# Two mixture-of-experts layers around attention: keeping the split weights of experts 11 to 15 in SBUF during the first layer

## What is computed

```python
x = x + 0.5 * moe(layernorm(x), norm_w, gate_w, gate_b, w1, b1, w2, b2)
x = x + attention(layernorm(x), w_q, w_k, w_v, w_o)
x = x + 0.5 * moe(layernorm(x), norm_w, gate_w, gate_b, w1, b1, w2, b2)

def moe(x, ...):                     # x: 2048 tokens of 256
    t = x * rsqrt(mean(x * x) + eps) * norm_w
    vals, idx = top_k(t @ gate_w.T + gate_b, 4)
    G = softmax(vals) scattered into (tokens, 16)
    h = einsum('mh,eoh->emo', t, w1) + b1        # 512 columns
    a, b = minimum(h[..., ::2], 7), clip(h[..., 1::2], -7, 7)
    act = a * sigmoid(1.702 * a) * (b + 1)       # 256 columns
    y = einsum('emi,edi->emd', act, w2) + b2     # 256 columns
    return x + einsum('me,emd->md', G, y)
```

## Time and profile before

| | us |
|---|---|
| median of 3 runs | 806.96 |
| lowest and highest run | 806.67, 808.38 |
| the profiled execution | 809.67 |
| its span in the profile | 807.9 |
| TensorE busy | 703.2 |
| VectorE (DVE) busy | 585.3 |
| ScalarE (ACT) busy | 439.8 |
| GpSimd (POOL) busy | 402.4 |

### The profile page before, as it was taken

One profiled execution on the slowest core, in us unless ns is written; L12 is line 12 of the kernel. 1 busy time (PEld: TensorE's weight loads), 2 busy tenths in 40 slices (PEclk: granted clock), 3 DMA queues, 4 the chain that ended last, 5 costly groups with the idle time before them and its releaser, 6 DMA issues.

```text
span 807.9 us, 17709 instructions
## 1 busy us (share of the span) xinstructions
PE 703.2 (87%) x4754; PEld 558.6 (69%) x4754; DVE 585.3 (72%) x1324; ACT 439.8 (54%) x1066; POOL 402.4 (50%) x449
## 2 busy tenths in 40 slices
PE   2576558989999999778999999998699999999995
PEld 1453336768888888666677777656478888888872
DVE  2868356877777777647779888857777777777777
ACT  3663334555555555426667676655345555555551
POOL 6667764445555555453234532447525555555552
PEclk9999978999999999999999999989999999999999
DMA  7779899998888773265444344137656778877676
GB/s 296 271 270 370 271 328 330 406 377 278 250 273 270 248 238 100 99 234 179 162 147 175 135 148 149 60 127 256 224 185 233 268 252 270 267 240 239 225 259 241
DMA packets 87420, 188.88 MB, mean 234 GB/s; under 512 B 13072, under 2 KB 37920, under 8 KB 85792
## 3 DMA queue, kind: packets, MB, share of 16 engines
q1 hardware_dynamic: 47680, 102.31, 37.4%
q0 software_dynamic: 14928, 49.97, 16.3%
q10 hardware_dynamic: 24720, 35.47, 13.4%
HBM read 105.46 MB, written 65.45 MB: 212 GB/s over the span
## 4 chain that ended last, share of the span: by engine, by line
PE 26%; POOL 11%; issue 10%; DVE 7%; DMA 1%; ACT 1%; SPq 0%; ACTq 0%; DVEq 0%; POOLq 0%
POOL kbuf L1283 6%; PE s_psT L1071 5%; PE s_psO L1656 3%; PE s_psS L1621 3%; DVE s_a_nm L1889 2%; PE s_psG L1593 2%; POOL rows L1514 2%; POOL s_e_own_bc L1295 2%; PE s_psG L1095 2%; PE s_psT L1637 1%; PE s_psT L1641 1%; PE s_psG L1606 1%; PE s_psG L1703 1%; PE s_psS L1038 1%; PE s_psG L1679 1%
## 5 line engine op out<-in xcount | busy, mean ns | idle before, releaser
L1283 POOL DMA_INDIRECT kbuf<-f_e_ys,f_e_place x79 | 79.2, 1003 | 99.0 <-ACT f_e_ys L1230 78.3
L1283 POOL DMA_INDIRECT kbuf<-s_e_own_ys,s_e_own_place x79 | 79.0, 1000 | 91.7 <-ACT s_e_own_ys L1230 78.7
L1071 PE MATMUL f_bank<-f_e_w,f_e_th 128*128 x316 | 121.1, 482 | 3.5 <-ACT f_e_th L1255 2.6
L1071 PE MATMUL s_psT<-s_e_own_w,s_e_own_th 128*128 x316 | 113.7, 461 | 2.0 <-ACT s_e_own_th L1255 1.8
L1514 POOL DMA_INDIRECT rows<-s_a_row,s_a_slot_i x64 | 63.7, 995 | 77.5 <-DVE s_a_slot_i L2016 60.5
L1889 DVE TENSOR_REDUCE s_a_nm<-s_psS 128x4 f32<-128x1024 f32 x64 | 78.2, 1222 | 27.1 <-PE s_psS L1621 26.8
L1136 DVE TENSOR_TENSOR s_e_own_hb<-s_psT,s_e_own_bias 128x512 f32<-128x512 f32 x79 | 54.3, 687 | 48.4 <-PE s_psT L1071 48.4
L1136 DVE TENSOR_TENSOR f_e_hb<-f_bank,f_e_bias 128x512 f32<-128x512 f32 x79 | 54.2, 687 | 45.4 <-PE f_bank L1071 45.3
L657 POOL DMA_INDIRECT rows<-f_r_row,f_r_slot_i x64 | 67.5, 1054 | 35.5 <-issue 17.9
L1071 PEld LDWEIGHTS f_bank<-f_e_w,f_e_th 128*128 128x128 f32 x316 | 63.3, 201 | 25.7 <-issue 7.4
L2155 ACT ACTIVATE s_a_pT<-s_psT 128x1024 f32<-128x1024 f32 x62 | 63.3, 1022 | 31.1 <-PE s_psT L1641 31.0
(11 more groups left out here) (383 smaller groups left out, 1804.7 us busy)
## 6 DMA issues: line engine op xcount, KB each, us to landing
f_e_w<-w_split SPq DMA_DIRECT2D x24, 512.0 KB, 5.1
...
s_e_tb<-rows ACTq DMA_DIRECT2D x80, 144.0 KB, 3.3
w_split<-stage ACTq DMA_DIRECT2D x7, 1536.0 KB, 7.8
f_e_tb<-rows ACTq DMA_DIRECT2D x66, 144.0 KB, 4.9
...
w_split<-stage POOLq DMA_DIRECT2D x5, 1536.0 KB, 7.3
...
```

What stands on the lines that cost most here:

```text
L1071: last = pe.matmul(psH[j][:, :], left[:, p % 2, j, k * P:(k + 1) * P], w1[:, bass.ds(buf, 1), h, k * I2:(k + 1) * I2], start=n == 0, stop= ...
L1283: pool.indirect_dma_start(out=kbuf[:, :], out_offset=bass.IndirectOffsetOnAxis(ap=place[:, i % KEPT:i % KEPT + 1], axis=0), in_=ys[:, n, : ...
```

## The change

Experts 11 to 15 are no longer reloaded in the first layer. They are loaded raw into places where they stay, split there, and used from there. All weights of the first layer lie in one array `weights` of 28 units of 1024 columns: nine units that were the three stage buffers, 13 of the ring, and six kept ones, which share their memory with the router's buffers. Experts 11 and 12 stay in stage buffers 1 and 2, 13 and 14 in the kept units, 15 in stage buffer 0. In the second layer the array has only the 13 ring units.

The five experts are still stored, since the second layer reads them, but at POOL's steps 16, 19, 22, 25 and 28 instead of 4, 6, 8, 9 and 11. The raw loads of 13 and 14 wait for no store now, that of 15 for the store of 10. SP waits at its end for the five stores, ahead of the fetch of the attention weights, which land in the ring's memory. Weight loads that were two DMAs are one.

The table's column with the expert's number now holds a packed word: the expert, the unit of its first weights shifted by 5, and that of its second weights shifted by 10. DVE computes it as a sum over steps. TensorE unpacks it with shifts and masks.

```diff
+UNIT = 1024
+SLOT, RING_UNITS, HOME_UNITS = 3, 13, 6
+RING_AT, KEPT_AT = 3 * SLOT, 3 * SLOT + RING_UNITS
+UNITS = KEPT_AT + HOME_UNITS
+SECOND_UNITS = (2, 5, 8, 11, 12)
+HOMES = {11: SLOT, 12: 2 * SLOT, 13: KEPT_AT, 14: KEPT_AT + SLOT, 15: 0}
+def spots(first_layer):
+    base = RING_AT if first_layer else 0
+    return [(HOMES[e], HOMES[e] + 2) if first_layer and e in HOMES else (base + SLOT * (e % 4), base + SECOND_UNITS[e % 5]) for e in range(NE)]
+def packed(first_layer):
+    return [e + (first << 5) + (second << 10) for e, (first, second) in enumerate(spots(first_layer))]
...
+    one.done(one.engine.tensor_tensor(tiles["passed"][:, :], tiles["past"][:, :], steps, ALU.mult))
     one.link(one.engine.tensor_tensor(tiles["pastn"][:, :], tiles["past"][:, :], tiles["nt"][:, :], ALU.mult))
+    one.done(one.engine.tensor_reduce(tiles["spot"][:, :], tiles["passed"][:, :], X_AXIS, ALU.add))
...
-        one.done(one.engine.tensor_copy(table[0:1, to:to + NT], psN[0:1, k * P:k * P + NT]))
+        one.done(one.engine.tensor_scalar(table[0:1, to:to + NT], psN[0:1, k * P:k * P + NT], float(first) if k == 1 else 0.0, None, ALU.add))
...
+    BEHIND = {7: 4, 8: 5, 9: 6, 10: 7, 11: 8, 12: 9, 15: 10}
...
     def load(self, queue, e):
-        if e - self.STAGED >= self.DIRECT:
-            queue.wait_ge(self.s_out[e - self.STAGED - self.DIRECT], 16)
-        if e >= self.DIRECT:
-            queue.dma_start(self.staged(e)[:, 1, :].bitcast(fp32), self.w_raw[e]).then_inc(self.s_in[e], 16)
-        else:
-            queue.dma_start(self.ring1[:, e, 1, :].bitcast(fp32), self.w_raw[e, :, 0:HID]).then_inc(self.s_in[e], 16)
-            queue.dma_start(self.ring2[:, e, 1, :].bitcast(fp32), self.w_raw[e, :, HID:WCOLS]).then_inc(self.s_in[e], 16)
+        if e in self.BEHIND:
+            queue.wait_ge(self.s_out[self.BEHIND[e] - self.DIRECT], 16)
+        queue.dma_start(self.columns((self.at(e) + 1) * UNIT, WCOLS).bitcast(fp32), self.w_raw[e]).then_inc(self.s_in[e], 16)
...
+            at = packed(layer == 0) + packed(layer == 0)[-1:]
+            for e in range(NE):
+                ch.done(dve.memset(c["steps"][:, layer, e:e + 1], float(at[e + 1] - at[e])))
...
     def load_first(sp, e):
-        for part in range(2):
-            sp.dma_start(w1[:, e % NBUF, part, :].bitcast(fp32), w_split[e, :, part, 0:HID]).then_inc(s_w1[e % NBUF], 16)
-        load_bias(sp, e, e % NBUF)
+        sp.dma_start(split.columns(at_unit[e][0] * UNIT, 2 * UNIT).bitcast(fp32), w_split[e, :, 0:2 * UNIT]).then_inc(s_w1[e % NBUF], 16)
...
-    ACT_STORES, POOL_STORES, POOL_LOADS, SECOND_LAG = {1: 8, 2: 9, 3: 10}, {4: 11, 6: 12, 8: 13, 9: 14, 11: 15}, {4: 13, 6: 14, 8: 15}, 2
+    ACT_STORES, POOL_STORES, POOL_LOADS, SECOND_LAG = {1: 8, 2: 9, 3: 10}, {16: 11, 19: 12, 22: 13, 25: 14, 28: 15}, {4: 13, 6: 14, 8: 15}, 2
...
         def next_first(e):
             sp.wait_ge(s_hb, tiles_before[e - NBUF])
             carry(sp, s_carrys)
-            if first_layer:
-                split.stored(sp, e)
-            load_first(sp, e)
+            if split.kept(e):
+                split.split(sp, e)
+                carry(sp, s_carrys)
+            else:
+                if first_layer:
+                    split.stored(sp, e)
+                load_first(sp, e)
+            load_bias(sp, e, e % NBUF)
             ready_first(sp, e)
         def next_second(e):
+            if split.kept(e):
+                sp.sem_inc(s_ready2, 1)
+                return
...
+        if first_layer:
+            sp.wait_ge(s_hb, tiles_before[9])
+            carry(sp, s_carrys)
+            sp.wait_ge(s_y, tiles_before[12] + 1)
+            carry(sp, s_carrys)
+            for e in HOMES:
+                split.stored(sp, e)
+                carry(sp, s_carrys)
...
-                e = expert(i)
-                buf = pe.snap(e % NBUF)
-                pe.wait_ge(s_ready1, e + 1)
+                spot = expert(i)
+                at = pe.snap((spot >> 5) & 31).with_bounds(min_val=0, max_val=len_units - SLOT)
+                pe.wait_ge(s_ready1, (spot & 31) + 1)
...
-                    last = pe.matmul(psH[j][:, :], left[:, p % 2, j, k * P:(k + 1) * P], w1[:, bass.ds(buf, 1), h, k * I2:(k + 1) * I2],
+                    last = pe.matmul(psH[j][:, :], left[:, p % 2, j, k * P:(k + 1) * P], weights[:, h:len_units + h - SLOT + 1, k * I2:(k + 1) * I2][:, bass.ds(at, 1), :],
...
-            e = expert(i)
-            buf = pe.snap(e % NSEC)
-            pe.wait_ge(s_ready2, e + 1)
+            spot = expert(i)
+            at = pe.snap(spot >> 10).with_bounds(min_val=0, max_val=len_units - 1)
+            pe.wait_ge(s_ready2, (spot & 31) + 1)
```

More of the change, by code:

```diff
@@ L621, in _ @@
                 one = Chain(dve, s_one)
-                tile_columns(one, c, tiles, hist[:, LAST + 1, :], None)
+                tile_columns(one, c, tiles, hist[:, LAST + 1, :], None, c["steps"][:, 0, :])
                 dve.sem_inc(s_cols, 1)
@@ L1026, in _ @@
         turn_over(pe, c, spare, FILL)
-        expert = Column(pe, "e", NT, NE - 1)
+        expert = Column(pe, "e", NT, most)
         def spread(p):
@@ L1118, in _ @@
         routed.table(dve)
-        expert = Column(dve, "e", NT, NE - 1)
+        expert = Column(dve, "e", NT, most)
         def low_parts(s, at):
@@ L1311, in __init__ @@
             place = lambda name, shape, dt: freed.enter_context(nc.sbuf_tensor(name, shape, dt))
-            self.stage = [place(f"stage{k}", [P, 2, WCOLS], fp32r) for k in range(Split.STAGED)]
+            self.weights = place("weights", [P, UNITS, UNIT], fp32r)[:, :, :]
         self.w_qkv, self.w_oT = w_qkv, w_oT
+        mem.sb("rest", [P, SLOT * UNIT], fp32)
         self.wp = mem.sb("wp", [P, 2, KC, 3 * D], fp32r)
@@ L2099, in _ @@
         one = Chain(dve, s_one)
-        tile_columns(one, c, tiles, hist[:, NG, :], hist)
+        tile_columns(one, c, tiles, hist[:, NG, :], hist, c["steps"][:, 1, :])
         dve.sem_inc(s_r["cols"], 1)
```

139 lines of the change are left out of this document (79 added, 60 removed).

## The result

The changed kernel takes 809.37 us (median of 20 runs, 805.62 to 814.11), the kernel before 806.31 us (20 runs, 800.18 to 809.97). The ratio is 1.0052, 95% interval 1.0033 to 1.0071: slower, where 3.5 us faster had been forecast. The medians differ by 3.1 us; a ratio here is an estimate of its own from the faster group of each kernel's runs, not the quotient of the medians, and 1.0052 of 806.31 us is 4.2 us. Measured a second time (e5) the ratio was 1.0049 (1.0017 to 1.0081).

A forecast was written before the change was run, and what follows sets the result against it. TensorE bounds the steady loops; only the first loop's early stretch, slowed by waits, could gain. 2.2 + 0.8 + 0.8 − 0.3 = 3.5 us faster, 803.5 us from the median 806.96 (chance 0.58); 8-in-10 range 798.5 to 808.4.

The forecast's parts named there:

- I take 41 ... Cost 0: TensorE's sequencer: eight added register instructions per pair at 41 ns, 0.33 us, hidden in its wait of 1182 or 661 ns.
- The rival "slower": Sequencer becomes the bound in pairs with table registers, both loops: at 146 ns an instruction 8 us lost, 811.5 us; chance 0.10.
- the traffic there is 259 GB/s before and after ... Cost 0: Steady first loop: moved stores replace dropped reloads of the same 7.86 MB; cost 0, bound one late tb fetch, 2.2 us.
- The gain, 3.8 us: First loop, 133 to 185 us, stores gone: 2.2 us token fetch, 0.8 raw load of expert 15, 0.8 register loads.
- The tb wait of 2.20 us: TensorE's wait at 175.95 us for a fetch of token rows; expected to go with fetches 3.3 us earlier, gaining 2.2 us.
- The rival "DVE is the bound": First loop's 133 to 185 us: DVE, not DMA, bounds it; at most 1.6 us gained, 806.2 us; chance 0.22.
- no change: Whole kernel within 0.2% (1.6 us) of before, 805.4 to 807 us, as DVE bounds the early stretch; chance 0.22.
- the 9.7 us: First loop, 139.18 to 184.66 us: seven pairs' 45.48 us against 35.7 at steady pitch, the most the change could find.
- much faster: All seven early pairs of the first loop come down to the steady pitch: 9.7 us gained, 797.3 us; chance 0.10.
- SP's new waits and the merged loads: SP's waits for the stores before the attention-weight fetch, and fewer, larger weight DMAs in both layers: cost 0 each.
- The test at 133 us: Sign of error: any difference over 0.3 us at 133 us, ahead of the moved stores, would show the forecast wrong in place.
- The table path: Tile table of both layers: two more small DVE instructions per layer, 0.3 us lost, bounds 0 and 0.7.

The follow-up runs named there:

- e5: The changed kernel as it is, measured a second time; ratio to the kernel before 1.0049 (1.0017 to 1.0081), median 808.39 us.
- e8: The changed kernel, still with shift and mask, its five stores moved to POOL's steps 13, 17, 21, 25, 29; ratio to the kernel before 1.0023, median 808.46 us.
- e6: The changed kernel with fused unpacking (divide and modulo) and stores at POOL's steps 13, 17, 21, 25, 29; ratio to the kernel before 0.9988, median 805.70 us.
- e2: The kernel before plus only the packed word unpacked by shift and mask, eight register operations more per pair, on a slower chip; ratio 1.0078 (1.0033 to 1.0122).
- e16: The kernel before plus only the eight added register operations per pair, measured again on another slower chip; ratio 1.0041 (1.0001 to 1.0080).
- e9: The kernel before, unchanged, profiled a second time; one execution of 803.48 us, pairs 5 to 12 in 43.0 us.

## Why the prediction was wrong, point by point

**The sequencer, "I take 41 ... Cost 0": the term that was mis-sized.** An added register operation held TensorE's sequencer 92 to 98 ns, not 41. The prediction had the mechanism, its place and the point from which it decides, 83 ns in pairs with a table load. It took a row's own duration for the distance to the next instruction, which no row of a group gives. At 98 ns eight of them took 0.79 us. That is inside the 1.18 us of most pairs and more than the 0.66 of a pair with a table load, where the wait fell to 51 ns. By the prediction's own formula this is 0.79 − 0.66 = 0.13 us in about 16 pairs, an estimate of 2 us. Priced by the profiles: 2.0 us in the first loop (e8 against e6), 0 to 0.7 in the second; by the ratios of e2 and e16 3.5 to 6.7 us in all, by their medians 0.4 to 2.5. The rival "slower" got 0.10; its mechanism is about half of what the steady loops lost, at a quarter to a third of its price of 8 us.

**The moved stores, "the traffic there is 259 GB/s before and after ... Cost 0": the mechanism that was missed.** Bytes were the wrong measure: in 200 to 300 us it was 260 GB/s and is 244. A register load of the table that began 1.5 to 5.3 us after the issue of a 1.5 MB store took 1.6 to 2.5 us in the steady loop instead of 0.6, and the prediction's own show it, in the stretch where the stores then stood; the text put them down to the traffic "or beside it" and never asked what comes later. It costs 2.3 us (changed against e8, by the profiles). The bound that was given, one fetch late, 2.2 us, was near in size and wrong in kind.

**The gain, 3.8 us: right in kind, too large here, and read from one late execution.** The tb wait of 2.20 us is gone and the fetches landed as forecast, but the second profile of the kernel before has no such wait either, nor the slow-clock stretches (0.98 for 0.90 in 133 to 185 us). The profiled execution stood 2.7 us above the median, and the prediction subtracted a stall from it that the median run need not have. Against e9 alone the changed kernel's stretch gained nothing (43.0 and 43.1 us); against the fused kernel (41.6) it is 1.4 us, so part of the gain may have gone to the sequencer in the same stretch. Over all profiles moving the stores is worth 1.7 us there on the faster chips and 4.7 on the slower ones: a stall that comes in some executions enters as its mean, not as its length in one.

**The rival "DVE is the bound": right about the place.** Spreading DVE's lows took the seven pairs to 36.4 us and the wait for al to 0.4. Its own sign, waits for al that are longer by what the tb wait lost, can't be read: they are 3.2, 4.1 and 4.0 us in the two profiles of the kernel before and in the changed kernel's. It was counted as a reason for "no change" and not as the way to the 9.7 us that the forecast called "much faster".

**Right:** DMA at 242 GB/s, tb at 3.4 us, SP's new waits and the merged loads without cost (e6's loops are at the pitch of before or below it: 5.09 for 5.106). The test at 133 us could not be made: pair 5 stood at 139.2 and 134.8 us in two profiles of the kernel before alone. The table path cost about 0.6 us (first addition of pair 0 at 92.4 and 92.1 us in the two profiles of the changed kernel, 91.5 and 91.8 before), for 0.3 forecast.

The sum as measured: −2.4 to +0.2 in the stretch (by which profile of the kernel before), +3.4 to 3.8 in the steady first loop, +0.6 in the second, +0.6 in the table: 2.2 to 5.2 us, which holds the 3.1 us of the medians and the 4.2 of the ratio. It can't be made sharper: pairs 0 to 5 take 47.7 and 43.0 us in the two profiles of the kernel before, and the time between the last pair of the first loop and the first of the second is 258.9 and 257.6 us there, 256.9 and 256.4 in the changed kernel, which no run explains.
